# The last task of a two-layer spectral filter: its rows in a buffer of their own, most of them loaded before the last inverse H

## The chip, the cores and the metric

One core of a Trainium2 chip runs the whole program. The metric is the device time of one execution in microseconds; the kernel before takes 525.05 us (median of 3 runs, 522.98 to 525.10).

## The reference, cut to what matters

The input `x` is (4, 45, 90, 384) in fp32: 4 images, H = 45, W = 90, 384 channels in 8 blocks of 48. Two layers follow one another, each a 2-D Fourier transform over (H, W), a two-matrix network per channel block with a soft threshold at 0.01, and an inverse transform added to the layer's input.

```python
f = jnp.fft.fft2(xf, axes=(1, 2), norm='ortho')            # layer 0; layer 1 uses rfft2 and keeps re and im
Xk = (f.real - f.imag)[:, :total, :total]                  # 23 frequencies along H and W
o1 = relu(einsum('bhwni,nio->bhwno', Xk, w1[0]) + b1[0])
o2 = einsum('bhwni,nio->bhwno', o1, w2[0]) + b2[0]
spec[:, :total, :total] = softshrink(o2, 0.01)
y = jnp.fft.ifft2(spec, s=(H, W), axes=(1, 2), norm='ortho').real + x
```

The kernel stays among the frequencies between the layers; in space it needs only the first forward and the last inverse transform.

## The kernel before, in words

The work is cut into 8 **tasks** (4 images by 2 halves of 192 channels), numbered 0 to 7. Every transform is a product on TensorE (PE) with a constant matrix, and between the transforms along W and along H the data goes through scratch in DRAM, since the axis that lies over the partitions changes.

- **Forward W** (`fwd`, 12 groups of 4 image rows a task, line 572) writes `scr_f`.
- A task then has 6 **steps** of up to 4 frequencies of W (48 steps, numbered 0 to 47; a task's last step has 3). Step s loads `bt` (line 297), does forward H (`a`), layer 0 (`c0`, `d0`), layer 1 (`c1`, `d1`), a transpose (`t`) and **inverse H** (`e`, line 694). ACT and DVE copy the product of `e` into `et` (lines 448 and 540), and SP stores `et` to `scr_i` (line 303, 90 partitions by 4 runs of 768 bytes, 270 KB).
- **Inverse W** (`inv`, line 605): each of a task's 12 groups g takes 4 image rows (g = 11 has one). Its input `jr` is loaded from `scr_i` in five sets of groups, 0-2, 3-5, 6-8, 9-10 and 11. A set is two loads (48 partitions each, runs of 1536 bytes; line 326), one for the first two image rows of each group and one for the others; set 4 is one load of 36 KB (line 322). Three `jr` buffers take the sets in turn. The product is added to the image `img` by DVE (line 551), and POOL stores every two groups to the output (line 378, 540 KB).

The order is written out by hand in `schedule()`: a list of events that each engine walks through, taking those that concern it, in that order; an engine waits on semaphores in its own program order. Each HBM transfer is issued by an engine's queue: SP issues most, POOL those of images, ACT a few at the start. The trace shows SP's transfers as queue q1 and POOL's as q0.

**The end of the order** is what the change touches. Groups of inverse W of task 6 are put between the parts of steps 46 to 48: g = 0 to 6. The other five, g = 7 to 11, are **held** until after `e` of step 47, the last inverse H. Every group of tasks 0 to 6 uses the PSUM pair P3 (two banks; the other pairs are P0, P1, P2), so that each waits for DVE's add of the group before it (lines 587 to 589). After the held groups come the five sets of task 7 (`rows`): set 0 waits for the stores of the last two steps, sets 0 to 2 for the `jr` buffer to be free of task 6's groups, and sets 3 and 4 go into the `bt` buffers. The 12 groups of task 7 use all four PSUM pairs in turn. Their adds are DVE's, but for g in `LAST_POOL` = (1, 4, 7, 10): ACT copies those to `p1` (line 456) and POOL adds them (line 386); `p1` is one buffer, so each copy waits for the POOL add before it. SP stores all 12 groups (line 330, 270 KB each, the last 67.5 KB) in order of g.

Of the kernel before, what the change touches and what calls it, by code (L numbers as in the profile page):

```python
# [15 lines left out]
KW, KWP = 23, 24  # L16
# [8 lines left out]
GROUPS = -(-H // 4)  # L25
XCH = 8
NXC = -(-H // XCH)
IMGS, FS, BT, JR = 3, 4, 3, 3
LAST_POOL = (1, 4, 7, 10)
# [73 lines left out]
def schedule():  # L103
# [50 lines left out]
def spectral_layers(nc, x, wts, const, out, where):  # L154
    ctx = ExitStack()
    with ctx:
# [31 lines left out]
        jr = [sb(f"jr{k}", [128, 3, 2 * HC]) for k in range(JR)]  # L188
        ps = ctx.enter_context(nc.psum_tensor("ps", [128, 8, 512], F32))
# [28 lines left out]
        j_tail = [sem(f"last_set{j}_loaded") for j in range(JR, len(JSETS))]  # L218
# [20 lines left out]
        def set_rows(t, j):  # L239

            if t == TASKS - 1 and j >= JR:
                return bt[j - JR][:, 0:(JSETS[j][1] - JSETS[j][0]) * 2 * HC].rearrange("p (g c) -> p g c", c=2 * HC)
            return jr[bank_of(t, j)[0]]
# [30 lines left out]
        def _(sp):  # L274
            sp.dma_start(cst[:, :], const).then_inc(c_ld, 16)
            for kind, *what in order:
# [28 lines left out]
                if kind == "rows" or (kind == "inv" and what[0] < TASKS - 1 and what[1] in (2, 5)):  # L305
                    t, j = what if kind == "rows" else (what[0], jset[what[1]] + JR)
                    k, used = bank_of(t, j)
                    landed = j_tail[j - JR] if t == TASKS - 1 and j >= JR else j_ld[k]
# [5 lines left out]
                    if t == TASKS - 1 and j >= JR:  # L314
                        sp.wait_ge(a_mm, 2 * NT)
                    elif used:
# [4 lines left out]
                    if g0 == GROUPS - 1:  # L321
                        sp.dma_start(set_rows(t, j)[0:2 * KWP, 0, 0:HC], rows[:, 4 * g0, :]).then_inc(landed, 16)
                    else:
                        four = rows[:, 4 * g0:4 * g1, :].rearrange("q (g r s) c -> q g r (s c)", r=2, s=2)
                        for r in range(2):
                            sp.dma_start(set_rows(t, j)[64 * r:64 * r + 2 * KWP, 0:g1 - g0, :], four[:, :, r, :]).then_inc(landed, 16)
                if kind == "inv" and what[0] == TASKS - 1:
# [3 lines left out]
            sp.wait_ge(y_last, 16 * GROUPS)  # L331

        @block.gpsimd
        def _(pool):
# [21 lines left out]
            for kind, *what in order:  # L356
# [24 lines left out]
                if kind == "inv" and what[0] == TASKS - 1 and what[1] in LAST_POOL:  # L381
# [4 lines left out]
                    nc.gpsimd.tensor_tensor(y, p1[0:W], y, ALU.add).then_inc(i_pool, 1)  # L386
# [7 lines left out]
        def _(act):  # L394
# [5 lines left out]
            for kind, *what in order:  # L400
# [42 lines left out]
                if kind == "e":  # L443
# [4 lines left out]
                    nc.scalar.activation(et[s % 2][0:2 * H, 0::2, :], ps[0:2 * H, P0, 0:2 * HC].rearrange("p (k c) -> p k c", c=HC), ACT.Copy).then_inc(e_act, 1)  # L448
                if kind == "inv" and what[0] == TASKS - 1 and what[1] in LAST_POOL:
                    t, g = what  # L450
                    n, B0 = LAST_POOL.index(g), 2 * (g % 4)
# [4 lines left out]
                    nc.scalar.activation(p1[0:W], ps[0:W, B0:B0 + 2, 0:2 * HC], ACT.Copy).then_inc(i_act, 1)  # L456

        @block.vector
        def _(dve):
# [4 lines left out]
            for kind, *what in order:  # L464
# [76 lines left out]
                if kind == "inv" and (what[0] < TASKS - 1 or what[1] not in LAST_POOL):  # L541
                    t, g = what
                    h0, h1 = hrows(g)
                    B0 = P3 if t < TASKS - 1 else 2 * (g % 4)
# [6 lines left out]
                    nc.vector.tensor_tensor(y, p, y, ALU.add).then_inc(i_add, 1)  # L551

        @block.tensor
        def _(pe):
# [8 lines left out]
            for kind, *what in order:  # L563
# [12 lines left out]
                if kind == "inv":  # L576
                    t, g = what
                    j = jset[g]
                    k, _ = bank_of(t, j)
                    if g == JSETS[j][0]:  # L580
                        if t == TASKS - 1 and j >= JR:
                            pe.wait_ge(j_tail[j - JR], 16 * set_dmas(j))
                        else:
                            pe.wait_ge(j_ld[k], rows_landed(t, j))
                    at = g - JSETS[j][0]
                    if t < TASKS - 1:
                        B0 = P3
                        vacate(0)
                        vacate(1)
                    else:  # L590
                        B0 = 2 * (g % 4)
                        if g < 4:
                            pe.wait_ge(i_add, t * GROUPS)
                            pe.wait_ge(t_add, 2 * NT)
                            pe.wait_ge(d0_ss, 2 * NT)
                            pe.wait_ge(e_act, NT)
                            pe.wait_ge(e_dve, NT)
                        elif g - 4 in LAST_POOL:
                            pe.wait_ge(i_act, LAST_POOL.index(g - 4) + 1)
                        else:  # L600
                            pe.wait_ge(*last_added(g - 4))
                    h0, h1 = hrows(g)
                    for r in range((h1 - h0 + 1) // 2):
                        n = min(2, h1 - h0 - 2 * r) * HC
                        last = mm(ps[0:W, B0 + r, 0:n], K["w_inv"][64 * r:64 * r + 64, :], set_rows(t, j)[64 * r:64 * r + 64, at, 0:n], start=True, stop=True)  # L605
# [112 lines left out]
```

## Time and profile before

| | before |
|---|---|
| median of 3 runs | 525.05 us (522.98 to 525.10) |
| the profiled execution | 524.21 us |
| its span, from the first to the last instruction | 522.4 us |
| PE busy | 478.2 us (92%) |
| DVE busy | 304.1 us (58%) |
| DMA moved | 104.63 MB, 200 GB/s on average |

Times in the trace count from the start of the span; the 1.8 us between span and execution time lie around it. A row of a timeline has start, length, engine, line, operation, tiles and shapes, how many instructions it merges, and in brackets the idle time before it with what ended that. A DMA-issuing row shows the time of issuing, not the transfer.

### The profile page before, as it was taken

How to read it: one execution, taken by the hardware profiler on the slowest of the kernel's cores; microseconds unless marked ns; L12 is line 12 of the kernel's file. 1: busy time of each engine (PE TensorE's matmuls, PEld its weight loads, DVE VectorE, ACT ScalarE, POOL GpSimd, SP SyncE). 2: the span in 40 equal slices, each digit the busy share in tenths (PEclk: the TensorE clock that was granted, in tenths of full speed). 3: DMA queues.
4: the chain of work that ended last, by engine and by line, in shares of the span. 5: the costliest groups of instructions: out<-in, count | busy, mean ns of one | idle time of the engine just before them, and what ended most of it. 6: DMA issues, size and time to landing. Idle time of an engine off the chain costs nothing.

```text
span 522.4 us, 14875 instructions
## 1 busy us (share of the span) xinstructions
PE 478.2 (92%) x6144; PEld 341.3 (65%) x6144; DVE 304.1 (58%) x674; ACT 209.1 (40%) x473; POOL 172.7 (33%) x194
## 2 busy tenths in 40 slices
PE   3639999999999999999999999999999999999763
PEld 1127778766776767766777777767776677786521
DVE  6324456456764577456763577456763577567643
ACT  0004555454345434454345434454345434444101
POOL 9803132212433234412433133412433222322134
PEclk9768999999999999999999999999999999999978
DMA  8758956386989578886989678896889655643497
GB/s 194 252 150 204 271 157 165 85 206 175 251 232 254 164 210 243 239 208 180 255 227 234 180 208 250 230 212 177 249 230 215 197 162 157 159 112 109 122 257 230
DMA packets 76720, 104.63 MB, mean 200 GB/s; under 512 B 7761, under 2 KB 63303, under 8 KB 76526
## 3 DMA queue, kind: packets, MB, share of 16 engines
q1 hardware_dynamic: 57622, 55.95, 40.2%
q0 software_dynamic: 10608, 40.45, 29.5%
q10 hardware_dynamic: 8424, 7.28, 5.3%
q8 instruction: 50, 0.82, 0.7%
q14 instruction: 16, 0.13, 0.1%
HBM read 52.21 MB, written 51.43 MB: 198 GB/s over the span
## 4 chain that ended last, share of the span: by engine, by line
PE 78%; DMA 7%; DVE 6%; POOL 3%; issue 2%; ACT 2%; SPq 1%; POOLq 0%; ACTq 0%; DVEq 0%
PE ps L669 13%; PE ps L605 12%; PE ps L694 12%; PE ps L572 11%; PE ps L656 11%; PE ps L618 8%; PE ps L681 4%; PE ps L634 4%; DMA scr_f<-fs 3%; PE ps L644 3%; DVE img L551 2%; DVE ns L525 2%; POOL xs L369 1%; ACT p L442 1%; DVE nt L503 1%
## 5 line engine op out<-in xcount | busy, mean ns | idle before, releaser
L551 DVE TENSOR_TENSOR img<-ps,img 90x768 f32<-90x768 f32 x92 | 82.6, 900 | 19.3 <-PE ps L605 15.7
L369 POOL TENSOR_TENSOR xs<-xs,nt 128x360 f32<-128x360 f32 (+1 forms) x48 | 41.6, 866 | 147.6 <-DVE nt L503 120.3
L605 PE MATMUL ps<-jr,cst 64*90 64x384 f32 (+1 forms) x358 | 80.2, 515 | 7.0 <-DVE img L551 5.7
L572 PE MATMUL ps<-img,cst 128*64 128x384 f32 (+1 forms) x368 | 73.8, 517 | 12.6 <-DMA img<-x 7.9
L378 POOL DMA_DIRECT2D y<-img x42 | 34.7, 825 | 131.9 <-DVE img L551 131.5
L618 PEld LDWEIGHTS ps<-cst,bt 128*64 128x64 f32 x1472 | 63.3, 141 | 20.4 <-issue 13.9
L435 ACT ACTIVATE o<-ps,wt 97x180 f32<-97x180 f32 (+1 forms) x96 | 33.8, 406 | 105.9 <-PE ps L656 105.9
L525 DVE SCALAR_TENSOR_TENSOR ns<-p,ps 109x384 f32<-109x384 f32 x96 | 53.1, 553 | 38.0 <-ACT p L442 33.0
L618 PE MATMUL ps<-cst,bt 128*64 128x90 f32 x1472 | 69.1, 248 | 5.9 <-DMA bt<-scr_f 5.9
L669 PE MATMUL ps<-wt,o 128*64 128x96 f32 x1472 | 73.9, 249 | 0.4 <-DVE o L517 0.4
L669 PEld LDWEIGHTS ps<-wt,o 128*64 128x64 f32 x1472 | 64.9, 137 | 12.6 <-issue 12.6
L694 PE MATMUL ps<-ns,cst 64*90 64x192 f32 x736 | 70.9, 322 | 0.0
L656 PE MATMUL ps<-xs,wt 64*97 64x180 f32 (+1 forms) x768 | 68.4, 315 | 2.4 <-POOL xs L369 2.1
L694 PEld LDWEIGHTS ps<-ns,cst 64*90 64x90 f32 x736 | 62.7, 155 | 8.4 <-issue 2.3
L656 PEld LDWEIGHTS ps<-xs,wt 64*97 64x97 f32 x768 | 57.3, 160 | 14.1 <-POOL xs L369 8.5
L442 ACT ACTIVATE p<-ps 109x384 f32<-109x384 f32 x96 | 47.1, 491 | 27.2 <-PE ps L669 27.2
L408 ACT ACTIVATE fs<-ps 112x384 f32<-112x384 f32 x84 | 38.9, 476 | 36.7 <-PE ps L572 27.0
L517 DVE TENSOR_SCALAR o<-ps,wt 97x180 f32<-97x180 f32 (+1 forms) x96 | 33.8, 394 | 33.0 <-PE ps L656 33.0
L572 PEld LDWEIGHTS ps<-img,cst 128*64 128x64 f32 x368 | 25.3, 143 | 41.7 <-issue 35.5
L488 DVE COPY xs<-ps 128x360 f32<-128x360 f32 (+1 forms) x48 | 24.8, 516 | 43.8 <-PE ps L618 43.8
L533 DVE TENSOR_TENSOR ns<-ps,ns 109x192 f32<-109x192 f32 x96 | 29.8, 352 | 33.5 <-PE ps L681 32.7
L362 POOL TENSOR_TENSOR xd<-xs 128x360 f32<-128x360 f32 (+1 forms) x48 | 38.1, 793 | 33.9 <-DVE xs L488 33.8
(41 smaller groups left out, 399.2 us busy)
## 6 DMA issues: line engine op xcount, KB each, us to landing
y<-img POOLq DMA_DIRECT2D x35, 540.0 KB, 5.6
img<-x POOLq DMA_DIRECT2D x30, 540.0 KB, 8.2
scr_i<-et SPq DMA_DIRECT2D x48, 270.0 KB, 5.7
scr_f<-fs SPq DMA_DIRECT2D x176, 72.0 KB, 3.3
bt<-scr_f SPq DMA_DIRECT2D x40, 270.0 KB, 5.0
jr<-scr_i SPq DMA_DIRECT2D x48, 216.0 KB, 5.2
img<-x ACTq DMA_DIRECT2D x10, 540.0 KB, 6.7
y<-img SPq DMA_DIRECT2D x11, 270.0 KB, 3.6
```

Of the source, the lines that this page charges most:

```text
L362: nc.gpsimd.tensor_tensor(xd[:, :, 0:kws(s) * H].rearrange("p q (k m) -> p q k m", m=H), xt[:, :, :, 0:H], xt[:, :, :, H:2 * H], ALU.subtr ...
L369: nc.gpsimd.tensor_tensor(re, re, nt[s % 2][:, :, 0:kws(s), 0:H], ALU.subtract).then_inc(re_ok, 1)
L408: nc.scalar.activation(fs[k][0:rows, 0:cols], ps[0:rows, P3 + g % 2, 0:cols], ACT.Copy).then_inc(f_cp, 1)
L442: nc.scalar.activation(p1[0:rows, p, :], ps[0:rows, P2 + p, 0:2 * HC], ACT.Relu).then_inc(d1_p, 1)
L525: nc.vector.scalar_tensor_tensor(out=ns[0:rows, p].rearrange("p n r c -> p (n r c)"), in0=p1[0:rows, p, :], scalar=2 * LAM, in1=ps[0:rows, ...
L551: nc.vector.tensor_tensor(y, p, y, ALU.add).then_inc(i_add, 1)
L572: last = mm(ps[64 * r:64 * r + 64, P3 + g % 2, 0:(b - a) * HC], K["w_fwd"], img[t % IMGS][:, a:b, :].rearrange("p h c -> p (h c)"), start= ...
L605: last = mm(ps[0:W, B0 + r, 0:n], K["w_inv"][64 * r:64 * r + 64, :], set_rows(t, j)[64 * r:64 * r + 64, at, 0:n], start=True, stop=True)
L618: last = mm(ps[64 * ab:64 * ab + 64, P0 + q, k * 2 * H:(k + 1) * 2 * H], bt[s % BT][:, at:at + 64], K["h_fwd"], start=True, stop=True)
L656: last = mm(ps[0:2 * BS + 1, P2 + ab, q * STEP * H:q * STEP * H + n], w1[k, im, 2 * f + q, :], xt[k, q, 0:kws(s), im * H:(im + 1) * H], st ...
L669: last = mm(ps[64 * r:64 * r + 64, P2 + p, b * 2 * BS:(b + 1) * 2 * BS], o11[:, b, 2 * p + r, :], w21[:, block_no(s // STEPS, b), :], star ...
L694: last = mm(ps[0:2 * H, P0 + r, p * HC:(p + 1) * HC], K[("h_inv_re", "h_inv_im")[im]][k, :], ns[k, p, :, im, :], start=im == 0, stop=im == 1)
```

## The change

Task 7 gets a buffer `tl` of its own (128 partitions, 12 groups by 384 values) in place of `jr` and `bt`. Its spare partitions are cleared by 12 memsets of DVE, one after each add of task 0's groups. Rows of `scr_i` are numbered 2 per frequency: steps 42 to 46 write the first 40 (`EARLY`), step 47 writes the last 6. The first 40 are loaded by an event `first_rows`, which stands in SP's order ahead of the store of step 47 and waits for the stores of steps 45 and 46: two loads of 40 partitions by 11 runs of 1536 bytes, and one of 40 runs of 768 bytes for g = 11. The last 6 rows are loaded by `last_rows` after the store of step 47 has landed, by SP (two loads) and ACT (one). Group 0 of task 7 waits for all of these. The held groups of task 6 take the pairs P2, P1, P3, P2, P1. `LAST_POOL` loses g = 10; ACT's copies alternate between `p1` and a free `et` buffer, and ACT stores the three groups of POOL, behind its third copy.

```diff
+HELD = 7
-LAST_POOL = (1, 4, 7, 10)
+LAST_POOL = (1, 4, 7)
+EARLY = 2 * STEP * (STEPS - 1)
...
         order += inv[s][0:1]
+        if s == NSTEPS + 1:
+            order.append(("first_rows",))
         if s > 1:
             order.append(("e", s - 2))
...
     order += held
-    order += [("rows", TASKS - 1, j) for j in range(len(JSETS))]
+    order.append(("last_rows",))
     order += [("inv", TASKS - 1, g) for g in range(GROUPS)]
...
+        tl = sb("tl", [128, GROUPS, 2 * HC])
...
+        def last_rows(r, k0, k1):
+            rows = scr_i[TASKS - 1].rearrange("k e h c -> (k e) h c")[k0:k1]
+            four = rows[:, 0:H - 1, :].rearrange("q (g r s) c -> q g r (s c)", r=2, s=2)[:, :, r, :]
+            return four, tl[64 * r + k0:64 * r + k1, 0:GROUPS - 1, :], rows[:, H - 1, :], tl[k0:k1, GROUPS - 1, 0:HC]
+        def held_no(t, g):
+            return g - HELD if t == TASKS - 2 else -1
+        def pair_of(t, g):
+            if t == TASKS - 1:
+                return (P0, P1, P2, P3)[g % 4]
+            return (P2, P1, P3)[held_no(t, g) % 3] if held_no(t, g) >= 0 else P3
...
# SP
+                if kind == "first_rows":
+                    sp.wait_ge(tl_clr, GROUPS)
+                    for n in (NT - 3, NT - 2):
+                        sp.wait_ge(e_st[n % 2], 16 * (n // 2 + 1))
+                    for r in range(2):
+                        four, to, one, to_one = last_rows(r, 0, EARLY)
+                        sp.dma_start(to, four).then_inc(tl_first, 16)
+                    sp.dma_start(to_one, one).then_inc(tl_first, 16)
+                if kind == "last_rows":
+                    sp.wait_ge(e_st[(NT - 1) % 2], 16 * ((NT - 1) // 2 + 1))
+                    four, to, one, to_one = last_rows(0, EARLY, 2 * KW)
+                    sp.dma_start(to, four).then_inc(tl_rest[0], 16)
+                    sp.dma_start(to_one, one).then_inc(tl_rest[0], 16)
-                if kind == "inv" and what[0] == TASKS - 1:
+                if kind == "inv" and what[0] == TASKS - 1 and what[1] not in LAST_POOL:
...
# ACT
+                if kind == "last_rows":
+                    act.wait_ge(e_st[(NT - 1) % 2], 16 * ((NT - 1) // 2 + 1))
+                    four, to, _, _ = last_rows(1, EARLY, 2 * KW)
+                    act.dma_start(to, four).then_inc(tl_rest[1], 16)
...
-                    if n > 0:
-                        act.wait_ge(i_pool, n)
+                    act.wait_ge(e_st[NT % 2], 16 * ((NT - 2) // 2 + 1))
+                    if n > 1:
+                        act.wait_ge(i_pool, n - 1)
+                    p = (p1[0:W], et[NT % 2][0:W].rearrange("p (r s) c -> p r (s c)", r=2))[n % 2]
...
+            for n, g in enumerate(LAST_POOL):
+                h0, h1 = hrows(g)
+                act.wait_ge(i_pool, n + 1)
+                act.dma_start(out[b, h0:h1, :, f * HC:(f + 1) * HC].rearrange("h w c -> w h c"), img[(TASKS - 1) % IMGS][0:W, h0:h1, :]).then_inc(y_last_act, 16)
...
# DVE, after the add of a group
+                    if t == 0:
+                        nc.vector.memset(tl[:, g, :], 0.0).then_inc(tl_clr, 1)
...
# PE, before a group of inverse W
+                    if t == TASKS - 1:
+                        if g == 0:
+                            pe.wait_ge(tl_first, 48)
+                            pe.wait_ge(tl_rest[0], 32)
+                            pe.wait_ge(tl_rest[1], 16)
...
+                        if n == 0:
+                            pe.wait_ge(d1_ss, 2 * NT)
+                        elif n == 1:
+                            pe.wait_ge(d0_ss, 2 * NT)
+                            pe.wait_ge(t_add, 2 * NT)
+                        elif n >= 3:
+                            pe.wait_ge(i_add, t * GROUPS + g - 2)
+                        else:
+                            vacate(0)
+                            vacate(1)
```

## Rows read from the trace of the kernel before

**Rows 1.** Chain of waits, 484 to 523 us: start, us, what

```profile
492.67 1.43 PE ps L694 x12
...
501.30 6.35 DMA jr<-scr_i
...
510.15 1.82 POOL img L386
...
515.76 1.80 POOL img L386
```

**Rows 2.** Timeline of PE, 486 to 525 us

```profile
495.90 0.88 PE L605 MATMUL ps<-jr,cst 64*90 64x384 f32 x4 [1.16 <-DVE img L551]
...
503.47 8.33 PE L605 MATMUL ps<-jr,cst 64*90 64x384 f32 x36 [0.49 <-issue]
```

**Rows 3.** Timelines of DVE and ACT, 486 to 525 us

```profile
494.80 0.95 DVE L551 TENSOR_TENSOR img<-ps,img 90x768 f32<-90x768 f32 x1 [0.24 <-PE ps L605]
...
503.01 0.35 DVE L551 TENSOR_TENSOR img<-ps,img 90x192 f32<-90x192 f32 x1 [1.10 <-PE ps L605]
...
506.37 0.81 ACT L456 ACTIVATE p<-ps 90x768 f32<-90x768 f32 x1 [11.69 <-PE ps L605]
```

**Rows 4.** Timeline of SP's queue, 486 to 525 us

```profile
488.56 0.32 SPq L303 DMA_DIRECT2D scr_i<-et  x1
...
494.71 0.32 SPq L303 DMA_DIRECT2D scr_i<-et  x1
497.34 6.76 SPq L326 DMA_DIRECT2D jr<-scr_i  x6
...
506.74 12.84 SPq L330 DMA_DIRECT2D y<-img  x12
```

**Rows 5.** DMA issues of 488.4, 440.3, 494.5 us and 455 to 523: KB, us to landing

```profile
scr_i<-et SPq DMA_DIRECT2D x1, 270.0 KB, 2.7
...
scr_i<-et SPq DMA_DIRECT2D x1, 270.0 KB, 6.3
...
scr_i<-et SPq DMA_DIRECT2D x1, 270.0 KB, 2.6
...
jr<-scr_i SPq DMA_DIRECT2D x1, 36.0 KB, 2.5
```

**Rows 6.** DMA packets, 452.8 to 453.4 us, then 453.5 to 459 us

```profile
DMA packets 138, 0.20 MB, mean 330 GB/s; under 512 B 9, under 2 KB 138, under 8 KB 138
...
DMA packets 750, 1.05 MB, mean 191 GB/s; under 512 B 72, under 2 KB 746, under 8 KB 750
```

**Rows 7.** DMA packets, 471.6 to 474 us, then 479.1 to 481 us

```profile
DMA packets 375, 0.28 MB, mean 115 GB/s; under 512 B 15, under 2 KB 375, under 8 KB 375
...
DMA packets 224, 0.30 MB, mean 155 GB/s; under 512 B 32, under 2 KB 224, under 8 KB 224
```

**Rows 8.** Timeline of POOL, 486 to 505 us

```profile
489.96 0.83 POOL L378 DMA_DIRECT2D y<-img  x1 [5.31 <-DVE img L551]
496.21 0.81 POOL L378 DMA_DIRECT2D y<-img  x1 [5.43 <-DVE img L551]
```

**Rows 9.** DMA queues, 501.6 to 504 us: packets, MB, share of 16 engines

```profile
q0 software_dynamic: 106, 0.44, 83.7%
q1 hardware_dynamic: 96, 0.14, 17.0%
```

**Rows 10.** Windows: us, busy (count) of PE, PEld, DVE, ACT, POOL, clock, DMA

```profile
503.50:507.50 4.00, 4.00 (x12) 1.57 (x12) 0.95 (x1) 0.81 (x1) 1.04 (x2) 0.51 1.01 284
507.50:510.00 2.50, 2.39 (x16) 1.21 (x16) 1.99 (x3) 0.73 (x1) 1.57 (x1) 1.00 0.93 323
```

**Rows 11.** DMA packets, 515 to 521.5 us

```profile
DMA packets 2257, 1.65 MB, mean 254 GB/s; under 512 B 105, under 2 KB 2257, under 8 KB 2257
```

**Rows 12.** Timeline of DVE, 0 to 30 us, then 124 to 152 us

```profile
5.99 1.02 DVE L463 MEMSET jr<- 128x1152 f32 x1 [0.30 <-issue]
...
136.07 0.55 DVE L540 COPY et<-ps 90x384 f32<-90x384 f32 x1 [0.42 <-PE ps L694]
```

More of the change, by code:

```diff
@@ L217, in spectral_layers @@
         j_ld = [sem(f"j{k}_loaded") for k in range(JR)]
-        j_tail = [sem(f"last_set{j}_loaded") for j in range(JR, len(JSETS))]
+        tl_clr, tl_first = sem("last_rows_spare_cleared"), sem("last_task_first_rows_loaded")
+        tl_rest = [sem(f"last_task_rest_rows{r}_loaded") for r in range(2)]
+        y_last_act = sem("y_of_last_task_stored_act")
         i_mm, i_add = sem("inv_product"), sem("inv_added")
@@ L307, in _ @@
                     k, used = bank_of(t, j)
-                    landed = j_tail[j - JR] if t == TASKS - 1 and j >= JR else j_ld[k]
                     if j == 0:
@@ L321, in _ @@
                     if g0 == GROUPS - 1:
-                        sp.dma_start(set_rows(t, j)[0:2 * KWP, 0, 0:HC], rows[:, 4 * g0, :]).then_inc(landed, 16)
+                        sp.dma_start(jr[k][0:2 * KWP, 0, 0:HC], rows[:, 4 * g0, :]).then_inc(j_ld[k], 16)
                     else:
@@ L325, in _ @@
                         for r in range(2):
-                            sp.dma_start(set_rows(t, j)[64 * r:64 * r + 2 * KWP, 0:g1 - g0, :], four[:, :, r, :]).then_inc(landed, 16)
-                if kind == "inv" and what[0] == TASKS - 1:
+                            sp.dma_start(jr[k][64 * r:64 * r + 2 * KWP, 0:g1 - g0, :], four[:, :, r, :]).then_inc(j_ld[k], 16)
+                if kind == "first_rows":
[12 more added lines that the diff above has]
+                if kind == "inv" and what[0] == TASKS - 1 and what[1] not in LAST_POOL:
                     g, (h0, h1), (b, f) = what[1], hrows(what[1]), divmod(TASKS - 1, HALVES)
@@ L385, in _ @@
                     y = img[t % IMGS][0:W, h0:h1, :].rearrange("p (r s) c -> p r (s c)", r=2)
-                    nc.gpsimd.tensor_tensor(y, p1[0:W], y, ALU.add).then_inc(i_pool, 1)
+                    p = (p1[0:W], et[NT % 2][0:W].rearrange("p (r s) c -> p r (s c)", r=2))[n % 2]
+                    nc.gpsimd.tensor_tensor(y, p, y, ALU.add).then_inc(i_pool, 1)
                 if kind == "load" and what[0] % STEPS == 3 and what[0] // STEPS >= 2:
@@ L577, in _ @@
                     t, g = what
[L578 to L595, printed above, removed]
+                    B0, n = pair_of(t, g), held_no(t, g)
+                    if t == TASKS - 1:
[3 more added lines that the diff above has]
+                            pe.wait_ge(tl_rest[1], 16)
                             pe.wait_ge(e_act, NT)
                             pe.wait_ge(e_dve, NT)
+                        elif g < 4:
+                            pe.wait_ge(i_add, (TASKS - 2) * GROUPS + max(m for m in range(HELD, GROUPS) if pair_of(TASKS - 2, m) == B0) + 1)
                         elif g - 4 in LAST_POOL:
@@ L601, in _ @@
                             pe.wait_ge(*last_added(g - 4))
+                    else:
+                        j = jset[g]
+                        k, _ = bank_of(t, j)
+                        if g == JSETS[j][0]:
+                            pe.wait_ge(j_ld[k], rows_landed(t, j))
+                        if n == 0:
[5 more added lines that the diff above has]
+                            pe.wait_ge(i_add, t * GROUPS + g - 2)
+                        else:
+                            vacate(0)
+                            vacate(1)
+                    rows = tl[:, g, :] if t == TASKS - 1 else jr[k][:, g - JSETS[j][0], :]
                     h0, h1 = hrows(g)
@@ L604, in _ @@
                         n = min(2, h1 - h0 - 2 * r) * HC
-                        last = mm(ps[0:W, B0 + r, 0:n], K["w_inv"][64 * r:64 * r + 64, :], set_rows(t, j)[64 * r:64 * r + 64, at, 0:n], start=True, stop=True)
+                        last = mm(ps[0:W, B0 + r, 0:n], K["w_inv"][64 * r:64 * r + 64, :], rows[64 * r:64 * r + 64, 0:n], start=True, stop=True)
                     last.then_inc(i_mm, 1)
```

18 lines of the change are left out of this document (7 added, 11 removed).

## The prediction

> **What bounds it now.** I read the page first (PE is busy for 92% of the span, so little outside a stage without PE work can be gained), then the chain of waits from 484 us on, then the engines' timelines, SP's queue and the DMA queues there. The chain shows PE's last inverse H ending at 494.1 us, held groups, then 6.35 us of waiting for a load of rows, then copies and adds of ACT and POOL to 517.6 us [rows 1]. PE shows why the held groups are slow: 0.88 us of products, then 1.16 us of waiting for an add, a group every 2.02 us [rows 2]; the last add ends at 503.36 us [rows 3]. Task 7 begins at 503.47 us, which I call T0 [rows 2], and the span ends 18.9 us later, at 522.4. The change acts on T0 and on the stretch D from T0 to the end. SP's queue gives the marks: the store of step 46 is issued at 488.56 us, that of step 47 at 494.71, the rows from 497.34 on [rows 4].
>
> **Held groups: 3 us earlier, off the path.** With other PSUM pairs their products no longer wait for the add before, except g = 9: its wait still names the group before it, whatever the pair. g = 7's add stays where it is, 494.80 to 495.75 [rows 3]. Then come g = 8's add, one cycle of 2.02 us for g = 9, one add of 0.97 for g = 10 and 0.35 for g = 11: the last ends near 500.05 us instead of 503.36. That pays only if task 7's rows are there by then.
>
> **When step 47's store lands.** This decides. `first_rows` stands ahead of that store on SP's queue. It waits for the store of step 46, which lands 2.7 us after 488.56 [rows 4, 5], so it issues at 491.25 us; with a start of about 1.1 us (an estimate: the second of rows 6 in which loads issued from 451.41 on run dense begins at 452.8) its bytes flow from 492.4. They are 40 x 11 x 2 x 1536 B + 40 x 768 B = 1.38 MB, and the store of step 47 with 0.28 MB comes behind them on the same queue: 1.66 MB before it has landed. Now a store of step 47 finds the queues empty and lands in 2.6 us [rows 5].
>
> How fast do they flow? No row shows loads of this size, so I bound it. The first load of a burst of the same 1536 B runs went at 330 GB/s; with five more behind it the burst went at 191 [rows 6]. A second thing counts. A lone store of 90 partitions leaves 375 packets of which 15 are small, two loads of 48 partitions leave 224 with 32 small [rows 7]: 15 and 16 end marks a transfer, so I read that a transfer is dealt out evenly over as many engines, up to 16, as divide its partitions. 40 partitions would then go over 10. The Trainium skill, "DMA: Bandwidth & Descriptors" (section "Why a DMA increments its semaphore by 16 and not by 1"), states this as the largest divisor up to 16; the trace agrees for 90 and 48, no run here yet shows 40. A run of 1536 B holds an engine for about 66 ns at the fast rate (0.6 us x 16 engines x 0.9 / 129 runs) and 130 ns in the burst: on 10 engines that is 233 or 118 GB/s. I take the middle, 180, near the burst's 191, which a deep queue of such loads resembles most.
>
> POOL's stores share the engines. One is issued at 489.96 and moves to about 493.8. The next is issued at 496.21, as now [rows 8], its bytes from 497.5; the other two now follow at once (g = 9's and g = 11's adds end at 498.7 and 500.05). With both queues at work q0 moved 0.44 MB and q1 0.14 MB in 2.4 us, about as many packets each [rows 9]: 183 against 58 GB/s. A store of `et` that met a POOL transfer took 6.3 us instead of 2.6 [rows 5]. So q1 moves 0.08 MB to 493.8, 3.7 x 180 = 0.67 to 497.5, and 0.46 in the 7.9 us that POOL's 1.45 MB then last, to 505.4. Of 1.66 MB 0.45 are left, 2 us more: 507.5. If q1 gets somewhat more in company, as in the tails of POOL's stores, it is 506. I take 506.8.
>
> **The last 6 rows and T0.** SP and ACT issue them on that landing. 36 KB landed in 2.5 us [rows 5]; this is 0.2 MB in three loads, two of them behind one another on SP: 2.9 us. T0 = 509.7, 6.2 us later than now.
>
> **D, the tail.** Nothing is loaded after T0 any more. PE has been idle since about 499. Now, after the gaps from 495.9 on, its granted clock was 0.51 of full speed from 503.5 to 507.5, so 1.2 GHz, then 1.00: three groups in 4.0 us, then four in 2.5 to 3.2 [rows 10]. I take the same: g = 7's product ends at T0 + 4.0 + 5 x 0.81 = T0 + 8.1, ACT's copy (0.81 [rows 3]) at T0 + 8.9. ACT's three stores stand behind this copy in its program, so the stores of g = 1 and 4 wait for it although POOL has added them. SP has sent five stores by then; 6.25 x 276 KB = 1.73 MB are left and go at 254 GB/s [rows 11], 6.8 us from T0 + 9.7: D = 16.6 us. POOL's chain (1.8 us an add [rows 1]), now three adds and overlapped with the copies, ends at T0 + 10.8 and sets nothing; that, and the loads gone from among the stores, is why D falls from 18.9. With the full clock from T0 on, D would be 1.3 us shorter; 15.4 to 17.4 are its ends.
>
> **The memsets.** 384 values are a third of 1152, which took 1.02 us [rows 12]: 0.4 us each, 4.8 for twelve if nothing covered them. DVE waits 0.42 us for PE after the add ahead of the copy to `et` [rows 12], and in the other two places of a step the next product comes later than DVE's delayed result. I take 0; it costs up to 0.4 where that slack is gone. Other edits (semaphores, the POOL group fewer) lie in these terms.
>
> **Sum.** T0 + 6.2, D - 2.3: +3.9 us on the profiled execution's 524.21, so 528.1; I say 528.0. The median is 0.84 above that execution, and +3.9 on it would be 528.9. About 0.5%, 2.6 us, is what a measurement can tell from no change.
>
> **Rivals.**
> - *The first rows are through before POOL's store comes (faster).* If they run at 330 GB/s as the burst's first load did [rows 6], 1.3 of 1.38 MB are in by 497.5, and step 47's store lands near 500, between its 2.6 and 6.3 us. T0 = 502.9, end 519.5, time 521.3. It decides at 330 GB/s and over; for it speaks that two large loads replace ten small ones, against it the burst's 191 and the 10 engines. The Trainium skill, "DMA: Bandwidth & Descriptors" (section "Rules for kernel authors"), asks for transfers of 1 MiB over 128 partitions for most bandwidth and for small ones to be merged; by that the rows gain. No row shows one so large. Chance 0.22.
> - *Earlier groups and later rows cancel (no change).* At 240 GB/s alone and 110 in company 0.97 MB are in by 497.5 and the remaining 0.69 by 503.8: T0 = 506.7, end 523.3, time 525.1. Chance 0.32.
> - *The burst's pace on 10 engines (much slower).* At 118 GB/s 0.52 MB are in by 497.5, 0.98 by 505.4; 0.40 of rows at 118 and the store take 4.5 us more: T0 = 512.9, end 529.5, time 531.3. Chance 0.13.
> - *The forecast*, 526.8 to 531, has 0.33.
>
> **How the numbers follow.** Slower by over 0.5%: 0.33 + 0.13 = 0.46; within: 0.32; faster: 0.22. The range reaches from the fast rival's 521 to the slowest's, 532 with D at 17.2; the forecast's own is 526.8 to 531.
>
> **What would show it.** Right: in SP's queue the store of step 47 still issued near 494.7 but landing after 8 us and more; small packets of `first_rows` that number 10 a transfer; POOL's three stores between 497 and 506 with q1 far below q0; PE idle from 499 to 508 and then at 0.5 of its clock; last stores on ACT's queue issued only after the third copy. Wrong: that store landing by 500, or PE beginning task 7 before 505. If instead the steps of task 1 have grown, the memsets were not covered.

## The result and the profile after

| | before | after |
|---|---|---|
| median | 525.02 us (522.98 to 525.10, 4 runs) | 536.15 us (534.80 to 538.79, 4 runs) |
| ratio, 95% interval | | 1.0228 [1.0181, 1.0274] |
| the profiled execution, its span | 524.21, 522.4 us | 534.80, 533.0 us |
| T0, where task 7 begins | 503.47 us | 515.35 us |
| D, from T0 to the end of the span | 18.9 us | 17.65 us |

The kernel is 2.3% slower, and 536.15 lies above the forecast's range of 521 to 532. The mechanism is the one forecast: step 47's store, behind the first rows, lands late, and T0 with it. Three sizes were off, all the same way. The chain of waits of the kernel after, 484 to 536 us (start, us, what), beside [rows 1]:

```profile
494.77 14.86 DMA scr_i<-et
509.63 0.02 issue
509.64 0.26 SPq L352
509.90 0.04 issue
509.95 5.32 DMA tl<-scr_i
515.26 0.09 issue
515.35 7.56 PE ps L653 x36
```

Two transfers in a row hold PE: the store takes 14.86 us where it took 2.6 [rows 5], then the last six rows 5.3 more. SP's queue in the same stretch, beside [rows 4]:

```profile
491.37 2.15 SPq L347 DMA_DIRECT2D tl<-scr_i  x2
493.57 0.66 SPq L348 DMA_DIRECT2D tl<-scr_i  x1
494.77 0.60 SPq L320 DMA_DIRECT2D scr_i<-et  x1
509.64 0.26 SPq L352 DMA_DIRECT2D tl<-scr_i  x1
```

The store is issued where it was (494.71 before): all the lost time lies between issue and landing. Its landing and those of POOL's stores, the last three of which took 5.3 to 6.5 us before, stand in the DMA issues from 491.5 to 509.6 us (KB, us to landing), beside [rows 5]:

```profile
y<-img POOLq DMA_DIRECT2D x2, 540.0 KB, 8.8
y<-img POOLq DMA_DIRECT2D x1, 337.5 KB, 8.5
scr_i<-et SPq DMA_DIRECT2D x1, 270.0 KB, 14.9
```

The PE timeline shows the held groups done early and PE idle for 16.71 us, where it began task 7 at 503.47 [rows 2]:

```profile
496.82 1.82 PE L653 MATMUL ps<-jr,cst 64*90 64x384 f32 x10 [1.37 <-DVE img L591]
515.35 9.15 PE L653 MATMUL ps<-tl,cst 64*90 64x384 f32 x46 [16.71 <-DMA tl<-scr_i]
```

DVE's timeline has the last three adds of the held groups; they end at 499.83, where the last one ended at 503.36 [rows 3]:

```profile
497.75 2.08 DVE L591 TENSOR_TENSOR img<-ps,img 90x768 f32<-90x768 f32 x3 [1.07 <-PE ps L653]
```

What the queues moved meanwhile (DMA queues of the kernel after, by window; q1 is SP's, q0 POOL's; packets, MB, share of 16 engines), one window after the other, for 494 to 497, 497 to 503, 503 to 506 and 506 to 509.6 us, beside [rows 9]:

```profile
q1 hardware_dynamic: 372, 0.47, 67.5%
...
q1 hardware_dynamic: 580, 0.85, 63.8%
q0 software_dynamic: 148, 0.59, 31.5%
...
q0 software_dynamic: 169, 0.65, 57.7%
q1 hardware_dynamic: 142, 0.15, 14.6%
...
q0 software_dynamic: 67, 0.21, 15.5%
q1 hardware_dynamic: 205, 0.16, 13.1%
```

Read them against the forecast's sum. Up to 503 SP's queue does better than forecast: 0.85 MB in six us beside POOL, 142 GB/s where the forecast had 58. But its last 0.31 MB take 6.6 us while it holds some 14% of the engines' time, about two engines of 16. A mean flow does not show that: the store has landed when its last engine is through.

The tail, after T0, in windows (us, busy and count of PE, PEld, DVE, ACT, POOL, clock, DMA share, GB/s), beside [rows 10]:

```profile
503.00:515.30 12.30, 0.00 (x0) 0.00 (x0) 0.00 (x0) 0.00 (x0) 0.00 (x0) 0.50 0.35 112
515.30:518.40 3.10, 3.05 (x10) 1.64 (x12) 0.95 (x1) 0.14 (x1) 0.00 (x0) 0.50 0.00 0
518.40:522.00 3.60, 3.60 (x24) 1.90 (x22) 2.81 (x4) 1.47 (x2) 2.57 (x2) 1.00 0.55 150
526.00:533.00 7.00, 0.00 (x0) 0.00 (x0) 0.00 (x0) 0.00 (x0) 0.00 (x0) 0.69 0.74 219
```

Task 7 starts at half clock as before, and from 526 us on only stores are left. ACT's third copy and POOL's last add (timelines of ACT and POOL) come early, where POOL's adds stood in the chain before [rows 1]:

```profile
522.29 0.81 ACT L490 ACTIVATE p<-ps 90x768 f32<-90x768 f32 x1 [1.13 <-PE ps L653]
...
523.18 1.80 POOL L414 TENSOR_TENSOR img<-p,img 90x768 f32<-90x768 f32 x1
```

The memsets cost nothing that can be told. Those shown on DVE's timeline (135 to 160 us) lie between an add and the next instruction; this one fills most of the 0.42 us for which DVE waited before the same copy [rows 12]:

```profile
136.09 0.38 DVE L593 MEMSET tl<- 128x384 f32 x1
136.47 0.55 DVE L580 COPY et<-ps 90x384 f32<-90x384 f32 x1
```

The stretch that holds all twelve, from DVE's copy to `et` in step 5 to that in step 17, took 117.12 us before and 117.60 here, but again 117.12 in the first run below, which has the same memsets.

### The profile page after: what moved, and what is told of

It reads as the page before. It is cut to its first block, busy times and chain, and to the rows that moved or that the text cites. A ratio compares the mean times of both kernels' runs of the same rounds, so it can differ in the third digit from the quotient of the medians.

```text
span 533.0 us, 14871 instructions
## 1 busy us (share of the span) xinstructions
PE 477.2 (90%) x6144; PEld 342.8 (64%) x6144; DVE 308.3 (58%) x687; ACT 208.4 (39%) x472; POOL 171.2 (32%) x193
## 4 chain that ended last, share of the span: by engine, by line
PE 81%; DMA 7%; DVE 5%; ACT 2%; POOL 1%; issue 1%; SPq 0%; DVEq 0%; POOLq 0%; ACTq 0%
PE ps L717 13%; PE ps L653 12%; PE ps L614 12%; PE ps L742 12%; PE ps L704 11%; PE ps L666 9%; PE ps L729 5%; PE ps L682 4%; PE ps L692 3%; DMA scr_i<-et 3%; DMA scr_f<-fs 2%; DVE ns L565 2%; ACT p L470 1%; POOL xs L396 1%; DVE nt L543 1%
## 5 line engine op out<-in xcount | busy, mean ns | idle before, releaser
L591 DVE TENSOR_TENSOR img<-ps,img 90x768 f32<-90x768 f32 (+1 forms) x93 | 83.1, 900 | 30.0 <-PE ps L653 26.3
L653 PE MATMUL ps<-jr,cst 64*90 64x384 f32 (+1 forms) x322 | 71.0, 502 | 2.7 <-DVE img L591 2.5
```

## The experiments

The question is why 1.38 MB of rows ahead of a 270 KB store hold it for 14.86 us, and what each other part of the change does. I call A: the store's place in SP's queue; B: POOL's stores, which now come together (issued at 496.27, 499.11 and 500.14); C: the bytes ahead of it; from the thirteenth run on H: the runs (contiguous pieces of 1536 bytes) that the fullest engine has to move first; the H and I of the eleventh run's expectation are others. "Store" is step 47's, from issue to landing, and T0 is counted from that issue as well. Both are read from one profiled execution of each kernel; where the loads around the store are the same (before and e5 to e7; e10 to e12), the store agrees within 0.1 us. A ratio compares with the kernel before on the same chip, whose median lay between 523.30 and 525.05 us; a row marked "1 run" has a single execution, whose time carries no verdict.

| run | store, us | T0, us after issue | median, us | ratio, 95% |
|---|---|---|---|---|
| before | 2.62 | 8.76 | 525.02 | |
| after | 14.86 | 20.6 | 536.15 | 1.0228 [1.0181, 1.0274] |
| e1_store_first | 2.85 | 16.3 | 532.17 | 1.0155 [1.0114, 1.0197] |
| e2_rows_32 | 6.60 | 13.95 | 529.33 | 1.0105 [1.0061, 1.0149] |
| e3_rows_on_act | 12.27 | 18.2 | 531.72 | 1.0148 [1.0106, 1.0190] |
| e4_no_pool_stores | 11.71 | 17.3 | 531.96 | 1.0152 [1.0096, 1.0209] |
| e5_held_only | 2.63 | 8.6 | 524.51 | 1.0018 [0.9993, 1.0043] |
| e6_pool_only | 2.63 | 9.85 | 523.60 | 1.0003 [0.9982, 1.0024] |
| e7_held_and_pool | 2.62 | 8.5 | 523.77 | 1.0000 [0.9970, 1.0030] |
| e8_rows_by_step | 4.93 | 10.95 | 525.17 | 1.0028 [1.0005, 1.0051] |
| e9_split_32_8 | 14.57 | 19.3 | 532.61 | 1.0189 [1.0139, 1.0239] |
| e10_behind_and_split | 3.44 | 9.05 | 523.65 | 1.0000 [0.9978, 1.0021] |
| e11_act_stores_early | 3.53 | 8.75 | 522.36 | 0.9983 [0.9959, 1.0007] |
| e12_pool_waits | 3.52 | 10.0 | 524.61 | 1.0024 [1.0005, 1.0043] |
| e13_rows_33 | 12.78 | 18.95 | 532.77 | 1 run |
| e14_rows_24 | 6.16 | 15.4 | 528.46 | 1 run |
| e15_split_no_pool | 10.05 | 14.6 | 528.81 | 1 run |
| e16_32_ahead_8_behind | 6.95 | 14.7 | 528.45 | 1.0078 [1.0050, 1.0106] |
| e17_rows_33_no_pool | 8.50 | 14.8 | 534.23 | 1 run |
| e18_rows_32_no_pool | 6.41 | 12.9 | 528.22 | 1 run |

**The store ahead of the rows.** In `schedule()` the event `first_rows` follows `e` of step 47:

```diff
-        if s == NSTEPS + 1:
-            order.append(("first_rows",))
         if s > 1:
             order.append(("e", s - 2))
+        if s == NSTEPS + 1:
+            order.append(("first_rows",))
```

> Edit: the event first_rows stands behind the store of step 47 in SP's order, not ahead of it; all else as changed. Theory A (queue order: the store of step 47 took 14.9 us because the 1.38 MB of first rows stand ahead of it on SP's queue): the store lands 2.6 to 3 us after 494.8, near 497.5; the last 6 rows are issued then, but SP's part of them now stands behind the first rows, which still need some 15 us (they were through only near 508 when issued at 491.4), so task 7 begins near 511 to 513 instead of 515.35 and the time falls by 2 to 4 us to about 531. Theory B (POOL's three stores hold up any transfer of SP then): the store still lands after 501 and more, as transfers that met a POOL store took 6.3 us. Theory C (bytes alone: all queues together moved 201 GB/s from 491.5 to 509.6, whatever the order): the store lands near 497.5 too, task 7 begins near 511.

Chain of waits of that run:

```profile
495.62 2.85 DMA scr_i<-et
...
498.79 13.04 DMA tl<-scr_i
```

With the loads behind it the store lands in 2.85 us: the loads ahead cause its 14.86. But T0 comes only 4.3 us sooner, since now the last rows stand behind the first on SP's queue and take 13 us. The rows themselves are slow, wherever they stand.

**Fewer rows ahead.** `EARLY` is 32; the last 14 rows follow the store.

> Edit: EARLY is 32 instead of 40, so the first rows are 32 partitions and the last rows 14; same place, same order. Theory A with engines (40 partitions were dealt over 10 engines, 92 runs each; 32 over 16, 46 runs each): the first rows are through near 498.5 to 500 and the store of step 47 lands at 501 to 503 instead of 509.6; the last rows, 14 over 14 engines, take 4 to 5 us more; task 7 begins near 506 to 508 and the time is 525 to 528. Theory C (bytes alone: 0.28 MB less ahead of the store at some 100 GB/s of this queue): the store lands near 507, task 7 begins near 512, time 531 to 532. The marks: first rows leave 16 small packets a transfer if the engine count is right, 10 if not.

20% fewer bytes of rows take 8.3 us off the store: not bytes alone (C). T0 is where A had it, but the median, 529.33, is above its 525 to 528, and the last 14 rows took 6.9 us instead of 4 to 5. What changed besides is the deal. Counting the small end marks on SP's queue between the issue of the rows and the store's landing gives 45 after (3 loads of 10, and 15 for the store) and 63 here (3 of 16, and 15): 40 rows went over 10 engines, 32 over 16.

**The rows on ACT's queue.** ACT issues the first rows in place of SP, at the same time.

> Edit: the same first rows at the same place in the order, but issued by ACT's queue instead of SP's, so that the store of step 47 has nothing of task 7 ahead of it on its own queue. Theory A (order within a queue): the store lands near 498 to 499 though the same bytes are under way on the other queue; task 7 then waits for the first rows, through near 507 to 508, and begins near 508.5, 7 us earlier than changed: time near 528. Theory B or C (the engines are full, whatever the queue): the store lands after 503, and task 7 begins at 512 or later.

The store, now alone on SP's queue, still takes 12.27 us and T0 comes at 513.23, as B and C had it, so A falls: it isn't the order within one queue. The DMA queues of this run from 495 to 500 us show the rows (q10) moving while the store (q1) crawls:

```profile
q10 hardware_dynamic: 523, 0.79, 66.0%
q0 software_dynamic: 54, 0.22, 13.7%
q1 hardware_dynamic: 125, 0.09, 6.2%
```

The 125 packets are 120 of the store, a third of its 360, and five marks: as many as 5 of its 15 engines hold, which I read as the five that the ten-engine loads leave free. The other 240 start only after 500 us. The Trainium skill, "DMA: Bandwidth & Descriptors" (section "Queues, rings and completion order"), says that the queues of SP and ACT are rings on the same 16 engines, that an engine drains a packet of many descriptors from one ring before it turns to the next, and that an end mark lands only after all earlier writes of its engine, whatever the queue. The trace agrees only in part. When the first of the 240 starts, at 500.44 us, 631 of the 880 long runs of the loads have started, some 63 for each of ten engines, far more than the 9 to 17 descriptors that the section calls typical of a packet; from then on the packets of the two queues come in about equal numbers (76 of ACT's and 70 of the store's from 501 to 502 us). Whether the marks were held back as well the trace does not tell.

**Without POOL's company.** POOL's last three stores of task 6 are left out (image rows 24 to 44 of that task are not stored).

```diff
+                    if t == TASKS - 2 and c >= 3:
+                        continue
                     pool.dma_start(out[b, r0:r1, :, f * HC:(f + 1) * HC]...
```

> Edit: as changed, but POOL's last three stores of task 6 (image rows 24 to 44 of that task) are left out. Theory A with engines: the first rows alone on 10 engines, 92 runs each at 100 to 130 ns, are through at 502 to 504.5, the store of step 47 lands near 503 to 505.5 instead of 509.6, and the rest (5.7 us to task 7's first product) is unchanged: task 7 begins near 509 to 511. Theory B (POOL's stores are the cause): the store lands by 499 and task 7 begins by 505. The difference to 509.6 is the price of the company: 4 to 6.5 us by A, over 10 by B.

POOL costs 3.15 us of the 14.86, so B, which had over 10, is not the main cause. A had 4 to 6.5 for it, and the landing without POOL by 505.5; it came at 506.04. DMA packets of this run, 494 to 506.1 us:

```profile
DMA packets 1274, 1.58 MB, mean 131 GB/s; under 512 B 46, under 2 KB 1274, under 8 KB 1274
...
q1 hardware_dynamic: 1273, 1.58, 59.2%
```

With nothing else on the engines SP's queue moves 131 GB/s and holds 59.2% of 16 engines, 9.5 of them. That is near the forecast's lower bound for ten engines, 118 GB/s, and far from the middle, 180. The last rows, alone here too, still took 5.14 us.

**The other parts of the change alone**, on the kernel before: the held pairs, POOL's part of the tail (three groups, two buffers, ACT's stores), and both.

> Edit: the kernel before with one part of the change alone, the PSUM pairs P2, P1, P3 for the five held groups of task 6. All loads stay as before. Theory D (the held groups were beside the path; task 7's first set of rows, which lands at 502.9 us, set its beginning): the last held add ends near 500 instead of 503.4, task 7 still begins at 503 to 503.5, the later sets are asked for some 2 to 3 us earlier but meet POOL's earlier stores; time 0 to 1.5 us shorter than before, inside what can be told. Theory E (the held groups set the end): 2.5 to 3.5 us shorter.

> Edit: the kernel before with the other part alone: three groups of task 7 for POOL instead of four, ACT's copies alternating between two buffers, and ACT storing POOL's groups behind its third copy. Theory F (the chain of ACT's copies and POOL's adds, 11.2 us from 506.4 to 517.6, set the end before): the last add ends near 515 instead of 517.6 and the time falls by 1 to 2.5 us, not more, since the 3.0 MB of stores then set the end at some 254 GB/s. Theory G (the stores set the end anyway, and ACT's three come late): within 0.7 us of before.

> Edit: the kernel before with both parts, held pairs and POOL's three groups, and the loads of task 7's rows as before (through jr and bt). If D and F hold, the two add up only as far as the loads allow: 1.5 to 3 us shorter than before, 520.5 to 522. If the loads of the first rows are all that was wrong with the change, this is the change without its fault and is faster than before by the 2.3 us by which I had put its tail shorter, or more.

None moves the time by what can be measured: D and G stand, E and F, by which it would move, fall, and the 1.5 to 3 us expected of both together did not come. With the held pairs T0 comes where it came, 8.5 to 8.6 us after the store's issue, since set 0's landing sets it (without them, in POOL's part alone, the last held add set it, at 9.85). Later sets land later. I put this down to POOL's last two stores, which start 4.3 and 5.4 us after the store's issue instead of 5.5 and 9.0 and share the engines; no run isolates it. In the run of both, the chain has:

```profile
498.88 9.18 DMA jr<-scr_i
```

**Rows step by step.** Each step's 8 rows are loaded ahead of the next step's store, so nothing large stands ahead of the last one.

```diff
+                    if t == TASKS - 1 and i > 0:
...
+                        for r in range(2):
+                            four, to, one, to_one = last_rows(r, 2 * STEP * (i - 1), 2 * STEP * i)
+                            sp.dma_start(to, four).then_inc(tl_first, 16)
```

> Edit: as changed, but the rows of each step of task 7 (8 partitions) are loaded just ahead of the store of the step after it, from step 43 on, when that step's own store has long landed; so only step 46's 8 rows stand ahead of the store of step 47. Theory A (what stands ahead of that store on the same engines sets its landing): the store lands within 3 to 4.5 us of 494.8, near 498; the last 6 rows take 5.3 us as in the change; task 7 begins near 503 to 504, 11 to 12 us earlier than changed; time 521 to 523. Rival: the loads of 8 partitions slow the loads of bt and the stores of steps 44 to 46, and PE waits there: the store of step 47 is issued 2 us or more later than 494.8.

T0 is 10.95 us after the store's issue instead of 20.6 and most of the loss is gone: 525.17 us, with an interval just above the kernel before. A, which had 521 to 523, is right in direction only: one set of 8 rows ahead still costs the store 2.3 us, and the last rows take 5.6. The rival's delay did not come: the store is issued at 495.74, not 2 us late.

**40 rows as 32 and 8.** Each first load is cut in two, in the same place.

> Edit: as changed, the same 1.38 MB of first rows at the same place on SP's queue, but each load of 40 partitions cut into one of 32 and one of 8. Theory A with engines (40 partitions went over 10 engines, 92 runs each; now 46 on 16 engines and 23 more on 8 of them): the busiest engine has 69 runs instead of 92, 23 x 0.13 = 3 us less, and meets POOL's stores for less long: the store of step 47 lands 10.5 to 12 us after its issue instead of 14.9, task 7 begins 3 to 4.5 us earlier, the time falls by as much, to 531.5 to 533. Theory C (bytes alone): 14.9 us stay, no change. Six loads instead of three cost at most 1.5 us more of issuing on SP, ahead of the store's issue only if they take longer than to 494.8.

If the number of engines of the large loads were all that counts, the store would land as with 32 rows; it took 14.57 us, C's 14.9 and not A's 10.5 to 12, though the time, 532.61, lay inside A's 531.5 to 533. Bytes and engines are told apart below. The marks number 87, 3 of 16, 3 of 8 and 15, so the deal was as meant. The eight engines of the small loads have 44 + 22 = 66 runs if they are among the 16, and the others 44.

**Rows behind the stores, and the tail.** In the first of three kernels each step's rows follow the next step's store and the last rows come in two parts, groups 0 to 3 first; the second also lets ACT store POOL's first two groups between its copies; in the third, POOL's last two stores of task 6 wait for the last rows.

> Edit: as in e8_rows_by_step, but the 8 rows of a step are loaded just behind the store of the next step instead of ahead of it, and the last 6 rows in two parts, groups 0 to 3 first, with task 7 beginning on these. Theory A: nothing stands ahead of the store of step 47, which lands in 2.6 to 3 us instead of 4.9; the first part of the last rows (24 runs a load on 6 engines) lands in 3.5 to 4.5 us instead of 6; task 7 begins 3 to 4.5 us earlier than in e8, the end comes 2.5 to 4 us earlier, time 521 to 522.5, 1 to 3 us faster than before. Rival: POOL's stores, which start at 497.5, now hold up both loads as long as before, and task 7 begins within 1.5 us of e8.

> Edit: e10_behind_and_split, and ACT stores the group that POOL has added after its next copy, not all three behind the third. If the late issue of these three was what kept the stretch from T0 to the end at 17.7 us (theory H), it falls to 16 to 16.8 us and the time by 1 to 1.6 us against e10; if the 3.0 MB of stores are limited by their rate once they flow (theory I), by less than 0.5.

> Edit: e11_act_stores_early, and POOL's last two stores of task 6 wait until the last rows have landed. If their company is what holds up the last rows, task 7 begins 1 to 2 us earlier than in e11; but their 0.9 MB then go among the 3.0 MB of task 7's stores, 3.3 us at 270 GB/s, of which the gap before the first of these (2.6 us after T0) takes most: time between 1.5 us faster and 1.5 us slower than e11.

The first falls short of A: the store takes 3.44 us instead of 2.6 to 3, T0 comes 1.9 us sooner than in e8 instead of 3 to 4.5, and 523.65 us is above 521 to 522.5. The second's mean is 0.8 us below the first's, between 1.9 faster and 0.4 slower, so its H and I can't be told apart. It is the best kernel of the study at 522.36 us, but its interval holds 1: it can't be told from the kernel before. Its chain:

```profile
492.43 3.53 DMA scr_i<-et
...
495.97 4.83 DMA tl<-scr_i
```

The store is 0.9 us slower than before, and the first part of the last six rows takes 4.8 (3.5 to 4.5 was expected). So even with nothing ahead T0 comes no sooner than before: what the early rows save, the slower landing of the last ones takes. Holding POOL's last two stores back did not help: T0, expected 1 to 2 us sooner than in the second, came 1.25 later, D was 20.2 us, and the median is 2.3 us above the second's. The profiled execution of the third was the slowest of its ten and that of the second nearly the fastest, so the two T0 compare loosely; but that the company of these two stores holds up the last rows is not shown.

**Bytes or the fullest engine.** 33 rows would go over 11 engines, 66 runs on each; 24 rows over 12, 44 on each, as many as 32 rows over 16.

> 33 first rows instead of 40, same place, the other 13 behind the landing. Beside the run with 32 rows (store of step 47 in 6.60 us) this adds 3% of bytes, but 33 partitions would be dealt over 11 engines with 66 runs of 1536 bytes each, where 32 went over 16 with 44 each. Theory H (the fullest engine sets it: its runs at 130 ns each, begun 2.3 us ahead of the store, then the store's own 2.6 us): 8.9 us without company, 9 to 12 with POOL's stores. Theory C (bytes): 6.6 to 7.6 us.

> 24 first rows, which would be dealt over 12 engines with 44 runs each, as many as with 32 rows, for three quarters of the bytes. Theory H: the store takes as long as with 32 rows, 6 to 6.8 us. Theory C (bytes): 3.5 to 5 us.

One row more than 32 lengthens the store from 6.60 to 12.78 us; eight fewer shorten it by 0.44. The marks, 48 and 51, are 3 of 11 and 3 of 12 and 15. C is out; H gave the order, but 12.78 is above its 12. The rest stands in the packets of the 33-row run from 501.1 to 506.8 us:

```profile
GB/s 399 356 361 366 264 437 334 357 259 388 426 426 226 329 361 226 329 199 291 232 232 162 232 265 162 102 38 38 38 0 38 38 0 38 11 22 22 0 0 0
DMA packets 342, 1.14 MB, mean 200 GB/s; under 512 B 60, under 2 KB 103, under 8 KB 342
...
q0 software_dynamic: 294, 1.10, 52.7%
q1 hardware_dynamic: 48, 0.04, 2.0%
```

The first line is the flow in 40 slices of the window: it sinks to 38 GB/s or nothing, single packets. In 5.7 us SP's queue moves 48. From 502.5 us on there are 27 of 768 bytes: 18 start one after another, most 0.21 to 0.22 us apart and each of 36 to 38 ns, between POOL's 4608-byte packets; when those end, nine follow 0.03 us apart. One engine of 11 holds 24 packets of the store and 3 of the third load of rows, 27 in all. The end marks fit: 44 of the 48 were there by 501.13 us, and the last four are as many as one engine leaves, the third of them behind the first three packets (503.18) and the fourth behind the other 24 (506.38). This one engine sets the landing.

**The same two loads without POOL's stores** (as above, image rows 24 to 44 of task 6 are not stored), and the cut loads as well:

> The first rows in loads of 32 and of 8 partitions (the store took 14.57 us so), and the last three POOL stores of task 6 left out (image rows 24 to 44 of it are not stored). The fullest engines have 44 + 22 = 66 runs. Theory H: 8.9 us, so that POOL's stores cost this order 5.7 us. Theory I (the small loads themselves are slow, whatever POOL does): 11 us or more. T0 follows the store by 5 us.

> 33 first rows (66 runs on the fullest of 11 engines) without POOL's last three stores of task 6 (image rows 24 to 44 of it are not stored). With those stores the last of the store's packets left one every 0.215 us, turn by turn with POOL's, from 502 to 506 us, 24 of them, which is what one engine holds. Theory J (an engine that is late with its rows pays for POOL's packets in turn, 24 times 0.18 us): without POOL the store lands after 8.5 to 9.5 us, 3.3 to 4.3 less than 12.78. Theory K (the deal over 11 engines is slow by itself): 11 us or more.

> 32 first rows (44 runs on each of 16 engines) without the same three stores. Theory J: the engines are through with the rows before POOL's packets pile up, so the store gains little, 5.5 to 6.4 us instead of 6.60; the step from 32 to 33 rows is then 2.5 to 3.5 us without POOL, where it was 6.2 with it. Theory K: the step stays 5 us or more.

| runs of 1536 bytes on the fullest engine | store alone, us | with POOL's stores, us | POOL's part, us |
|---|---|---|---|
| 44 (32 rows) | 6.41 | 6.60 | 0.2 |
| 66 (33 rows) | 8.50 | 12.78 | 4.3 |
| 66 (32 and 8) | 10.05 | 14.57 | 4.5 |
| 88 (40 rows, as changed) | 11.71 | 14.86 | 3.15 |

Alone, 22 runs more cost 2.1 to 3.6 us, and 44 more 5.3, 0.12 us a run; this is H. The step from 32 to 33 rows is 2.1 us without POOL (J had 2.5 to 3.5, K 5 or more) and 6.2 with it, so J holds but for its size, and K falls: an engine that is through before POOL's packets pile up pays almost nothing, one that isn't takes turns with them. For the cut loads H had 8.9 alone; 10.05 lies between it and I's 11, so small loads may cost something of their own, which no run isolates. The run with 33 rows and no POOL stores was some 6 us late already where the store was issued (499.82), and its whole time is not used.

**32 ahead, 8 behind the store.**

> 32 rows ahead of the store, the 8 rows of step 46 behind it, 6 rows after its landing. If the 8-partition loads ahead of the store undid the gain of 32: store in 6 to 7 us, T0 at 12 to 13.5 us after its issue, time 527 to 529. If the 8 rows behind it go on to hold the last rows as long as all rows behind the store did (T0 16.3 us after it): time 530 to 532.

The store takes 6.95 us, so the 8-partition loads ahead were what undid the cut. T0 at 14.7 is over the 12 to 13.5 expected: the last rows, behind 8 others, take 7.3. The time, 528.45, is as expected.

## Why the prediction was wrong

Point by point, the profiled execution against the forecast:

- **Held groups off the path: right.** Their last add ended at 499.83 (forecast 500.05) and bought nothing; alone, with 524.51 us, they change nothing either.
- **The store waits behind the first rows: right as to the mechanism, mis-sized.** It landed at 509.63, forecast 506.8: 2.8 us of the miss. The failed step is "I take the middle, 180", and with it the sum of bytes over queues that gave 507.5. Ten engines were right. But alone they ran near the lower bound, at 131 GB/s, and beside POOL SP's queue got 142, not 58. The run without POOL prices the two: at 180 GB/s and without company the store would have landed 6.9 us after its issue, and it took 11.71; the company, which had the other 5.2 us of the forecast, cost 3.15. The second error hid part of the first, by luck. What the sum also lacked is that bytes being in does not land the store. At 506 us 1.51 of 1.67 MB were in, and the rest took 3.6 us on about two engines' worth of time, until 507.9 in turns with POOL. The sum has a slip besides: its last 0.45 MB at 180 GB/s take 2.5 us, not 2, which makes 507.9 of 507.5. The rival with the burst's pace gave 509.9, nearly the landing, with 0.13 of chance; its flow in company, 58 GB/s, was as wrong.
- **The last 6 rows: mis-sized.** Landing to T0 was 5.7 us, forecast 2.9: 2.8 us more. The failed step takes the nearest row to be the 36 KB load of 48 partitions [rows 5]. Six partitions go over six engines: the window from 509.7 to 515 us of the kernel after has 18 marks for three loads.

```profile
DMA packets 156, 0.21 MB, mean 39 GB/s; under 512 B 18, under 2 KB 156, under 8 KB 156
...
q1 hardware_dynamic: 84, 0.11, 10.9%
q10 hardware_dynamic: 72, 0.10, 10.7%
```

  Nothing else is moving, and it is 39 GB/s. 22 runs on each of six engines at 0.12 us, on top of the small load's 2.5, are 5.1 us by an estimate from these rows. The same three loads with nothing beside them took 5.3 us here and 5.1 without POOL's stores, but 4.3 and 4.1 behind the cut loads (e9 and e15), so the estimate is rough. The prediction had found the rule of the deal, and used it for the 40 rows but not for the 6.
- **D: 17.65, forecast 16.6.** Loads out of the tail and POOL's adds overlapped: right, POOL's last add ended at T0 + 9.6 and set nothing. 1.81 MB of stores were left at T0 + 9.7 (forecast 1.73), and moved no slower than [rows 11]: the kernel after has, from 523 to 531.5 us,

```profile
DMA packets 3117, 2.29 MB, mean 269 GB/s; under 512 B 135, under 2 KB 3117, under 8 KB 3117
```

  The failed step ends the span when the bytes should be in, at T0 + 16.6: the last packet started at T0 + 16.9, and the span ended 0.74 us after it, as before (0.75). The full clock came at T0 + 3.1, not 4.0.
- **The memsets: right.** 0.38 us each, and the stretch with all twelve is no longer in the first run than before. The stores of steps 46 and 47 are issued 0.07 and 0.06 us later than before, which alone would show little: the second mark lies anywhere from 492.4 to 499.8 us in the runs.
- **The sum.** T0 +11.9 instead of +6.2, D -1.25 instead of -2.3: +10.6 on the span instead of +3.9; the three misses, 2.8, 2.8 and 1.05 us, make the difference. The medians are 11.1 us apart, since the profiled executions lie 1.4 us (after) and 0.8 us (before) below them. Slower had 0.46 of the chance; the range ended at 532 because it took the slow end of the flow, and of D, but never the slow end of the last rows.
- **Both milder rivals are out.** Rows through by 497.5 would have needed 330 GB/s; SP's queue had moved 0.51 MB at 497, and T0 came 8.7 us after the "cancel" rival's.

What stays open: the runs do not say why a 1536-byte run costs 0.12 us in these loads when the first 0.6 us of a burst go at 66 ns [rows 6], why in the 33-row run just one engine was late, nor why POOL cost 88 runs less (3.15 us) than 66 (4.3).

## What to carry to other kernels

Before a load is merged or moved ahead of something urgent, divide its partitions into engines (here the largest divisor up to 16): the time to count is the runs on the fullest engine, not the bytes, and 33 partitions can be far worse than 32. A transfer that someone waits for lands with its last engine, so anything large on the same engines delays it, from any queue, and another engine's traffic that comes before that engine is through adds its packets in turn. Work that is freed earlier than its successor can start is worth nothing, and its stores may then fall on the transfer that decides.

## What the runs showed of the hardware that I had not expected

- One partition more, 32 to 33, took the store from 6.60 to 12.78 us. The Trainium skill, "DMA: Bandwidth & Descriptors" (section "Why a DMA increments its semaphore by 16 and not by 1"), deals a transfer over the largest divisor of its partitions up to 16, from the lowest-numbered engine on. The end marks agree with the divisor for 40, 33, 32, 24, 8 and 6; the engines' numbers no run here shows.
- Another queue is no way round: 12.27 us from ACT's against 14.86 from SP's.
- Loads of 0.2 MB by six partitions with nothing beside them took 4.1 to 5.3 us in four runs (39 GB/s in the kernel after); a load of 36 KB by 48 partitions took 2.5 [rows 5].
- A 768-byte packet that takes turns with POOL's 4608-byte ones on one engine leaves every 0.21 to 0.22 us; alone, every 0.03.
